# Dense attention: the shift rows turned by VectorE in 32-blocks and copied by ScalarE in four steps, instead of transposed on TensorE

## What is computed

```python
qkv = jnp.einsum("bnd,ed->bne", x, W_qkv)
...
attn = jnp.einsum('bhnd,bhmd->bhnm', q, k) * scale
...
attn = attn + _spatial_bias(spatial_centers, N, x.dtype)[None, None]
attn = jax.nn.softmax(attn, axis=-1)
out = jnp.einsum('bhnm,bhmd->bhnd', attn, v)
```

## Time and profile before

| | us |
|---|---|
| median of 3 runs (lowest, highest) | 2945.84 (2945.65, 2948.85) |
| the profiled execution | 2948.08 |
| its span | 2946.3 |
| TensorE busy in the span | 2906.1 (99%) |
| VectorE busy | 2329.2 (79%) |
| ScalarE busy | 2272.1 (77%) |
| GpSimd busy | 1111.0 (38%) |
| mean granted TensorE clock | 0.994 of full speed |

### The profile page before, as it was taken

How to read it: one execution, slowest core, us unless ns; L and a number is a source line. 1 busy time by engine, 2 the same in 40 slices (tenths; PEclk the granted TensorE clock), 3 DMA queues, 4 the chain that set the end, 5 groups by cost and what they waited for, 6 DMA issues and landing times.

```text
span 2946.3 us, 107801 instructions
## 1 busy us (share of the span) xinstructions
PE 2906.1 (99%) x44672; PEld 1911.6 (65%) x44672; DVE 2329.2 (79%) x4219; ACT 2272.1 (77%) x4379; POOL 1111.0 (38%) x1835
## 2 busy tenths in 40 slices
PE   8999999999999999999989999999999999999998
PEld 4455555555555555555557777777777777777776
DVE  8888888888888889888857677677777667767775
ACT  4599999999999999999966666666666666666664
POOL 5411121122122211211145555555555554555554
PEclk9899999999999999999999999999999999999999
DMA  7631111111111111111121111111111111111110
GB/s 232 213 112 39 49 49 41 46 49 49 38 49 49 44 39 49 49 43 44 44 66 42 32 38 32 47 45 36 32 38 37 47 45 33 33 35 42 47 43 5
DMA packets 157392, 154.80 MB, mean 53 GB/s; under 512 B 17794, under 2 KB 130946, under 8 KB 156930
## 3 DMA queue, kind: packets, MB, share of 16 engines
q1 hardware_dynamic: 156930, 148.15, 16.1%
HBM read 89.37 MB, written 58.72 MB: 50 GB/s over the span
## 4 chain that ended last, share of the span: by engine, by line
PE 95%; DVE 3%; issue 1%; ACT 1%; SPq 0%; DMA 0%; POOL 0%; POOLq 0%; DVEq 0%; ACTq 0%
PE banks L1551 29%; PE banks L1487 15%; PE banks L1449 15%; PE banks L1504 15%; PE banks L1618 4%; PE banks L1566 4%; PE banks L1656 4%; PE banks L1585 3%; PE banks L1633 2%; PE banks L1643 1%; PE banks L1474 1%; DVE xn L1090 1%; DVE pair_max L1146 0%; DVE xn L1080 0%; PE banks L1731 0%
## 5 line engine op out<-in xcount | busy, mean ns | idle before, releaser
L1146 DVE TENSOR_REDUCE pair_max<-banks 128x1 f32<-128x1024 f32 x1024 | 1220.1, 1222 | 146.1 <-PE banks L1449 116.2
L914 ACT ACTIVATE probs<-banks 128x512 f32<-128x512 f32 x2048 | 1159.8, 599 | 63.8 <-PE banks L1487 5.4
L1487 PE MATMUL banks<-q_aug,k_aug 98*32 98x512 bf16 x8192 | 1144.5, 381 | 0.8 <-ACT probs L914 0.4
L1449 PE MATMUL banks<-k_aug,q_aug 96*32 96x512 bf16 x8192 | 820.3, 383 | 5.2 <-ACT v_all L881 3.3
L1504 PE MATMUL banks<-probs,v_cur 128*32 128x256 f32 x8192 | 796.9, 379 | 0.2
L1487 PEld LDWEIGHTS banks<-q_aug,k_aug 98*32 98x32 bf16 x8192 | 392.1, 95 | 197.4 <-ACT probs L914 5.1
L1504 PEld LDWEIGHTS banks<-probs,v_cur 128*32 128x32 f32 x8192 | 366.9, 111 | 166.5 <-ACT acc_sb L895 0.8
L643 POOL TENSOR_SCALAR row_max<-pair_max 128x1 f32<-128x1 f32 x508 | 131.9, 281 | 887.8 <-DVE pair_max L1146 887.8
L1449 PEld LDWEIGHTS banks<-k_aug,q_aug 96*32 96x32 bf16 x8192 | 310.6, 97 | 218.1 <-DVE pair_max L1146 11.0
L1551 PEld LDWEIGHTS banks<-hnT,w_sb 128*64 128x64 f32 (+1 forms) x5632 | 307.8, 137 | 25.2 <-ACT hnT L997 25.2
L1551 PE MATMUL banks<-hnT,w_sb 128*64 128x128 f32 (+1 forms) x5632 | 323.2, 275 | 0.9 <-ACT hnT L997 0.9
(11 more groups left out here) (144 smaller groups left out, 4033.2 us busy)
## 6 DMA issues: line engine op xcount, KB each, us to landing
acc_scratch<-acc_sb SPq DMA_DIRECT2D x128, 256.0 KB, 2.4
heads_win<-acc_scratch SPq DMA_DIRECT2D x512, 64.0 KB
q_aug<-q_parts SPq DMA_DIRECT2D x192, 64.0 KB, 2.2
k_aug<-k_parts SPq DMA_DIRECT2D x192, 64.0 KB, 2.2
q_parts<-parts SPq DMA_DIRECT2D x16, 384.0 KB, 3.1
k_parts<-parts SPq DMA_DIRECT2D x16, 384.0 KB, 4.0
x_in<-in_x SPq DMA_DIRECT2D x10, 512.0 KB, 4.9
xT_scratch<-xnT SPq DMA_DIRECT2D x8, 512.0 KB, 5.2
```

The source lines that it names most:

```text
L914: nc.scalar.activation(probs[:, step % PRING, :], banks[:, ring(h, use), :], ACT.Exp, scale=SCALE).then_inc(prob_ready, 1)
L1146: nc.vector.tensor_reduce(pair_max[:, group % 2, q, half:half + 1], banks[:, 4 + 2 * (t % 2):6 + 2 * (t % 2), :], AX.XY, ALU.max).then_inc ...
L1449: last = nc.tensor.matmul(banks[m:m + CT, 4 + t % 4, :], q_aug[0:TERM_ROWS, b, q * P + m:q * P + m + CT], k_aug[0:TERM_ROWS, b, kq * BANK: ...
L1487: last = nc.tensor.matmul(banks[m:m + CT, ring(h, use), :], k_aug[0:AUG, b, kb * P + m:kb * P + m + CT], q_aug[0:AUG, b, qc * CHUNK:(qc + ...
```

## The change

- TensorE no longer transposes the shift rows, and the identity in bf16 goes. Its ring of three banks counts steps alone; for SP the same points of the program are counted anew.
- `shift` and a new tile `shift_rows` are 128x4x32 bf16. GpSimd clears `shift` once and writes columns 0 and 1 of each 32. VectorE transposes all of it in 32x32 blocks (`turn_shift`, L1165 of the changed kernel), after the reduce of step 7. In `shift_rows` the two rows of the queries 32g to 32g+31 of each block of 128 then lie on partitions 32g and 32g+1, for g from 0 to 3.
- ScalarE copies them in four instructions (L891 of the changed kernel), each from partitions 32g and 32g+1 to partitions 96 and 97, 4x32 elements each, one behind the exponential of each of the steps 11, 12, 13 and 14. TensorE waits for all four before step 0.
- GpSimd joins the first three maxima as soon as their pairs are reduced.

```diff
-MSTEP = 13
+TURN = 32
+TURNS = P // TURN
+SAVE_STEP = 11
...
-        shift = sb("shift", [P, QC, SHIFT_ROWS], BF16)
+        shift = sb("shift", [P, QC, TURN], BF16)
+        shift_rows = sb("shift_rows", [P, QC, TURN], BF16)
...
+            nc.gpsimd.memset(shift[:], 0.0).then_inc(shift_zeroed, 1)
+            pool.wait_ge(shift_zeroed, 1)
...
             def split_max(h, group):
-                pool.wait_ge(smax_read, h * PAIRS + ((group + 1) * (PAIRS // GROUPS) + 2))
-                pool.wait_ge(shift_saved, h * GROUPS + group)
                 for q in range(QC):
+                    pool.wait_ge(smax_read, h * PAIRS + (group * (PAIRS // GROUPS) + 2 * (q + 1) + 2))
                     last = nc.gpsimd.tensor_scalar(row_max[:, q:q + 1], pair_max[:, group % 2, q, 0:1],
                                                    pair_max[:, group % 2, q, 1:2], None, ALU.max)
                 last.then_inc(max_step, 1)
                 pool.wait_ge(max_step, h * (2 * GROUPS) + (2 * group + 1))
+                pool.wait_ge(shift_turned, h * GROUPS + group)
                 nc.gpsimd.tensor_copy(shift[:, :, 0], row_max[:]).then_inc(max_step, 1)
                 pool.wait_ge(max_step, h * (2 * GROUPS) + (2 * group + 2))
                 nc.gpsimd.tensor_tensor(shift[:, :, 1], row_max[:], shift[:, :, 0], ALU.subtract).then_inc(shift_ready, 1)
...
-            def save_shift(group, bank):
+            def save_shift(h, group, g):
                 b, qc = (group // QC) % B, group % QC
-                nc.scalar.copy(q_aug[TERM_ROWS:AUG, b, qc * CHUNK:(qc + 1) * CHUNK],
-                               banks[TERM_ROWS:AUG, bank, 0:CHUNK // 2].bitcast(BF16)).then_inc(shift_saved, 1)
+                cols = q_aug[TERM_ROWS:AUG, b, qc * CHUNK:(qc + 1) * CHUNK].rearrange("s (j g c) -> s j g c", j=JT,
+                                                                                      c=TURN)
+                act.wait_ge(shift_turned, h * GROUPS + (group + 1))
+                nc.scalar.copy(cols[:, :, g, :], shift_rows[g * TURN:g * TURN + SHIFT_ROWS]).then_inc(shift_saved, 1)
...
             nc.scalar.sem_inc(acc_saved, 1)
-            act.wait_ge(st_ready, 1)
-            save_shift(0, 0)
+            for g in range(TURNS):
+                save_shift(0, 0, g)
             act.wait_ge(dist_scale, 1)
...
                 for step in steps:
-                    group, kb, use = step // KB, step % KB, use_of(step)
+                    group, kb = step // KB, step % KB
                     if ends and step >= STEPS:
...
                         continue
-                    act.wait_ge(st_ready, h * ST_USES + (use + 2 - (ends and step > STEPS - KB + MSTEP)))
+                    act.wait_ge(st_ready, h * STEPS + (step + 1))
                     act.wait_ge(pv_done, h * PVH + (1 if step < PRING else (step - PRING) // 4 * 2 + 3))
-                    nc.scalar.activation(probs[:, step % PRING, :], banks[:, ring(h, use), :], ACT.Exp,
+                    nc.scalar.activation(probs[:, step % PRING, :], banks[:, ring(h, step), :], ACT.Exp,
                                          scale=SCALE).then_inc(prob_ready, 1)
-                    if kb == MSTEP and not (ends and group + 1 == GROUPS):
-                        act.wait_ge(st_ready, h * ST_USES + (use + 3))
-                        save_shift(group + 1, ring(h, use + 1))
+                    if SAVE_STEP <= kb < SAVE_STEP + TURNS and not (ends and group + 1 == GROUPS):
+                        save_shift(h, group + 1, kb - SAVE_STEP)
                     if kb == SUMS_STEP and group > 0:
...
                 dve.wait_ge(max_step, 1)
+                dve.wait_ge(shift_zeroed, 1)
                 nc.vector.tensor_copy(shift[:, :, 0], row_max[:]).then_inc(max_step, 1)
...
                 nc.vector.tensor_tensor(shift[:, :, 1], row_max[:], shift[:, :, 0], ALU.subtract).then_inc(shift_ready, 1)
+
+            def turn_shift(h, group):
+
+                dve.wait_ge(shift_ready, h * GROUPS + (group + 1))
+                if h * GROUPS + group > 0:
+                    dve.wait_ge(shift_saved, (h * GROUPS + group) * TURNS)
+                nc.vector.transpose(shift_rows[:].rearrange("p j c -> p (j c)"),
+                                    shift[:].rearrange("p j c -> p (j c)")).then_inc(shift_turned, 1)
...
             first_shift()
+            turn_shift(0, 0)
             dve.wait_ge(dist_red, 2)
...
             for h, steps, ends in turns():
                 for step in steps:
                     tile = step + LEAD
-                    if ends and tile >= STEPS:
+                    if tile % 2 == 0 or ends and tile > STEPS + 1:
                         continue
-                    if tile % 2 == 1:
+                    if not (ends and tile >= STEPS):
                         max_pair(h, tile // 2)
+                    if tile // 2 % (PAIRS // GROUPS) == 0:
+                        turn_shift(h, tile // 2 // (PAIRS // GROUPS) - 1)
             dve.wait_ge(smax_read, HEADS * PAIRS + 2)
             nc.vector.sem_inc(phase2_end, 1)
             dve.wait_ge(phase2_end, 4)
...
-            def shift_rows(h, group, use):
-
-                pe.wait_ge(shift_ready, h * GROUPS + (group + 1))
-                bank_free(h, use)
-                if h == 0 and group == 0:
-                    pe.wait_ge(identb_set, 1)
-                for j in range(JT):
-                    last = nc.tensor.transpose(
-                        banks[TERM_ROWS:AUG, ring(h, use), j * P // 2:(j + 1) * P // 2].bitcast(BF16),
-                        shift[:, j, :], identb[:])
-                last.then_inc(st_ready, 1)
-
             def scores_to_exp(h, step):
-                group, kb, use = step // KB, step % KB, use_of(step)
+                group, kb = step // KB, step % KB
                 b, qc = (group // QC) % B, group % QC
                 if kb == 0:
-                    pe.wait_ge(shift_saved, h * GROUPS + (group + 1))
-                bank_free(h, use)
+                    pe.wait_ge(shift_saved, (h * GROUPS + group + 1) * TURNS)
+                if h * STEPS + step >= SRING:
+                    pe.wait_ge(prob_ready, h * STEPS + (step - SRING + 2))
                 for m in range(0, P, CT):
-                    last = nc.tensor.matmul(banks[m:m + CT, ring(h, use), :],
+                    last = nc.tensor.matmul(banks[m:m + CT, ring(h, step), :],
                                             k_aug[0:AUG, b, kb * P + m:kb * P + m + CT],
...
-            for t in range(KB):
-                max_tile(0, t)
-            shift_rows(0, 0, 0)
-            for t in range(KB, LEAD):
+            for t in range(LEAD):
...
-                    if kb == MSTEP and not (ends and group + 1 >= GROUPS):
-                        shift_rows(h, group + 1, use_of(step) + 1)
```

More of the change, by code:

```diff
@@ L41 @@
 LEAD = KB + 10
-MSTEP = 13
+TURN = 32
+TURNS = P // TURN
+SAVE_STEP = 11
 PRING = 16
 SRING = 3
-ST_USES = STEPS + GROUPS
 PAIRS = STEPS // 2
@@ L107, in build @@
         ident = keep("ident", [P, P], F32)
-        identb = keep("identb", [P, P], BF16)
         wqkv_sb = keep("wqkv_sb", [P, LAYERS, 2, 3 * INNER], F32)
@@ L216, in build @@
         minus_set = sem("minus_set")
-        identb_set = sem("identb_set")
+        shift_zeroed = sem("shift_zeroed")
         dist_step = sem("dist_step")
@@ L253, in build @@
         shift_ready = sem("shift_ready")
+        shift_turned = sem("shift_turned")
         shift_saved = sem("shift_saved")
@@ L376, in chunks, with ring @@
                 yield NCHUNK - 2 + u, NCHUNK // 2 - 1, u, u == 0, False
[L378 to L384, removed]
+        def ring(h, step):
+            return (h * STEPS + step) % SRING
         def turns():
@@ L520, in _ @@
                     if group == QC - 1:
-                        sp.wait_ge(st_ready, h * ST_USES + (STEPS // 2 + GROUPS // 2 + 1))
+                        sp.wait_ge(st_ready, h * STEPS + STEPS // 2)
                         load_aug(next_head, 0)
                     if group == GROUPS - 1:
-                        sp.wait_ge(st_ready, h * ST_USES + (ST_USES + 1))
+                        sp.wait_ge(st_ready, h * STEPS + STEPS)
                         load_aug(next_head, 1)
@@ L923, in _ @@
             act.wait_ge(prob_ready, HEADS * STEPS + 1)
-            act.wait_ge(shift_saved, HEADS * GROUPS)
+            act.wait_ge(shift_saved, HEADS * GROUPS * TURNS)
             nc.scalar.sem_inc(phase2_end, 1)
@@ L1100, in _ @@
             nc.vector.sem_inc(rest_ready, NMB)
-            dve.wait_ge(pool_const, 2)
-            nc.vector.tensor_copy(identb[:], ident[:]).then_inc(identb_set, 1)
             for u in range(2):
@@ L1453, in max_tile @@
                     last.then_inc(smax_ready, 1)
-            def bank_free(h, use):
-                if h * ST_USES + use < SRING:
-                    return
-                if use < SRING:
-                    h, use = h - 1, use + ST_USES
-                group, kb = divmod(use - SRING, KB + 1)
```

(23 more changed lines are left out.)

## The result

The changed kernel takes **3042.03 us** (median of 4 runs, 3040.96 to 3045.46) beside 2946.3 for the kernel before (4 runs, 2945.65 to 2948.85): a ratio of 1.0326, with a 95% interval of 1.031 to 1.0341. It is slower by 95.7 us. The forecast was 3045 in a range of 2996 to 3078. The profiled execution took 3045.46 us, its span is 3043.7 against 2946.3, the mean granted clock 0.993 against 0.994.

A forecast was written before the change was run, and what follows sets the result against it. TensorE was taken as the bound at 10.65 us per group; 3.70 + 0.54 + 7.19 makes 11.43, 0.78 more in 127 groups, +99 us: 3047 on the profiled execution, 3045 us against the median, range 2996 to 3078.

The forecast's parts named there:

- TensorE as the bound: Attention stage: 48 fours (sets of four matmuls) take 10.42 of 10.65 us per group; removing transposes gains 29 us at most.
- c: Duration of one of the four new copies on ScalarE: 0.29 us, bounds 0.211 and 0.366.
- Seams of +0.02 us: ScalarE, step 11's exponential to the fourth copy's end: seven gaps of +0.02 us between instructions, other bound -0.10 (overlap).
- The stretch of 3.70 us: ScalarE, start of step 11's exponential to the fourth copy's end: 4 x 0.60 + 7 x 0.02 + 4 x 0.29 us.
- From the copy's end to the end of step 0's four, 0.54: Handing over from ScalarE's fourth copy to the end of TensorE's step 0 scores: 0.54 us.
- From there to step 11's exponential: From the end of step 0's scores to the start of step 11's exponential: 7.19 us, as before the change.
- The period: Time of one group in the attention stage: 11.43 us instead of 10.65, 0.78 more in each of 127 groups.
- VectorE's transpose hidden: VectorE, behind step 7's reduce: any transpose under 1.0 us is hidden from ScalarE; without ScalarE's lateness, a tenth or two per group.
- Rival 1: ScalarE's seams: nothing is held, all overlap; stretch 2.86 us, period 10.59, time 2937 us; chance 0.09.
- Rival 2: ScalarE's seams: only a changed input partition in the same memory holds; period 11.07, +53 us, time 2998 us; chance 0.11.
- Rival 3: TensorE's clock falls in the new idle time, losing hundreds of us; chance 0.04 together with anything unseen.
- spreading is what costs: ScalarE's spread copies each end the overlap twice between exponentials, the last after step 14's; +99 us in total.

The follow-up runs named there:

- e9: Changed kernel with GpSimd making the four copies, and its maxima and copies at a head change issued before the wait for sums: 2918.68 us, ratio 0.9902.
- e1: Changed kernel with the four copies reading partitions 0 and 1 and writing partitions 0 and 1 of a spare tile: 2935.18 us.
- e3: Changed kernel with all four copies reading partitions 0 and 1, still writing partitions 96 and 97: 3045.21 us.
- e7: Changed kernel with GpSimd making the four copies behind VectorE's transpose, ScalarE keeping only the very first four: 2923.40 us, ratio 0.992.
- e8: Changed kernel with VectorE making the four copies behind its transpose, before the reduce of step 9: 3048.94 us.
- e2: Changed kernel with the copies reading partitions 32g and 32g+1 as before, but writing partitions 0 and 1 of a spare tile: 2997.58 us.
- e6: Changed kernel with all four copies directly behind each other after the exponential of step 11: 2968.20 us.

## Why the prediction was right

- **TensorE as the bound, 10.42 us of fours, 29 us to gain.** Borne out: e9 has the change without the copies on ScalarE and gains 28.4.
- **c = 0.29 us.** Measured 0.294. The bounds 0.211 and 0.366 were wider than needed.
- **Seams of +0.02 us, seven of them.** Measured 0.024 each. In the prediction this rested on three seams of the kernel before; e1 to e3 show it as a cause: the same copies cost nothing where no start changes.
- **The stretch of 3.70 us** measured 3.73. **From the copy's end to the end of step 0's four, 0.54**, is where the sum was most off: 812.35 + 0.40 - 812.30 = 0.45. In the row that it was read from, the weights and matmuls started 0.11 and 0.14 us after the copy's end (unrounded records), in the change 0.05; why is not shown. **From there to step 11's exponential**, 7.19 was taken over from the kernel before; it is 808.57 - (800.95 + 0.40) = 7.22. **The period** came out at 11.41 instead of 11.43, the span 97.4 us longer instead of 99. That it came so near is partly luck: the 0.09 us too many, 11 us in 127 groups, stand against 0.03 us too few in each of the two other terms. TensorE's wait reads 0.8 where about 1 us was said; its end in the trace is modelled, and the periods give 11.41 - 10.42 = 0.99.
- **VectorE's transpose hidden.** The kernel's row shows 0.30 us, the 311 ns of the Trainium skill ("VectorE: DVE Perf Modes", The three transpose paths) within 4%, and no one waits for it. e7 and e9 show it free without ScalarE's lateness too, where the prediction allowed a tenth or two per group; e8 shows where the cover ends.
- **Rival 1** (nothing held, 2937): wrong for this change, but e1 is that case and takes 2935.18. The rule of the Trainium skill that back-to-back ACTIVATEs overlap by about 93 ns ("ScalarE: Activation LUTs", What ACT_TABLE_LOAD costs) matches e1's -0.093 us between exponentials and copies, and fails at every seam of the change, where a start changes. **Rival 2** (only the input counts, 2998): wrong for this change too, and e2, which changes the input alone, takes 2997.58. By their own sums the two totals should read 2938 and 2999, which changes nothing. The rule that the Trainium skill has for VectorE, input and output both ("VectorE: DVE Perf Modes", Two Vector instructions with no wait between them), is what e1 to e3 show on ScalarE.
- **Rival 3** (the clock falls): no. The granted clock stays 1.00 in the window with TensorE idle for 20.2 of 300 us.

That spreading is what costs, the held seams and the late fourth copy taken together as the prediction had it, is shown by e6: together at the same step, the same copies lose 21 us against the kernel before, not 96. And the change's idea is sound: moved to an engine that nobody waits for, it gains 1%.

## What to carry to other kernels

A short instruction on a busy engine costs more than its own duration: here 0.29 us became 0.29 + 2 x (0.024 + 0.093) = 0.53, because it started at other partitions than its neighbours and ended the overlap on both sides. Before moving work off the engine that bounds, write down the stretch between the last input and the handing over on the new engine, seams included, and compare it with the break-even (2.92 us here). And ask first which engine has room: GpSimd, busy for 57 of 300 us, took the four copies for nothing.

## What the runs showed of the hardware

That a change of the output's starting partition alone holds ScalarE (e3) was not to be seen in the kernel before, nor that the input's is counted for PSUM and SBUF apart (e2: the exponentials behind the copies overlap them, and the first copy of a group is held by what the fourth of the group before read). VectorE has the same kind of seam: in e8 its copies, each from other input partitions, follow one another 0.031 us after the end of the one in front, while like instructions of its stream overlap by 0.084 us (unrounded records). The transpose, which overlaps the reduces by about 0.08 us on both sides in the change, starts 0.031 us after the reduce's end in e8, behind copies that read other partitions and wrote partition 96. The same copy of 2x128 bf16 took 293 to 299 ns on ScalarE where it was held, whatever the partitions (e2's held first copies read and write at partition 0), and 281 where it overlapped an exponential (e1); 284 on GpSimd, and (0.85 - 3 x 0.031) / 4 = 0.19 us on VectorE.
